# Two transformer layers in float32 on one core: another order of instructions at both ends of the two later attentions

## The chip, the cores and the metric

The kernel runs on one core of a Trainium2 chip. The metric is the device time of one execution in microseconds (us), the median of several runs. The engines are TensorE (PE in the profile, its weight loads apart as PEld), VectorE (DVE), ScalarE (ACT), GpSimd (POOL) and the queue that issues the DMAs (SP). Each runs its own list of instructions in order; semaphores tie the lists together.

## The reference

4096 tokens (2 sequences of 2048) of 256 numbers go through three blocks, all in float32. Block A is attention over a window of 128 with 16 heads and an MLP with GELU, followed by a layer norm of input plus output. Then come two layers B, each an attention with 8 heads of 64 and rotated keys and queries, and a gated MLP:

```python
def _layer(x, wqkv, qs, ksc, wo, lg, lb, w1, b1, w2, b2):
    h = shift_token(x)
    qkv = h @ wqkv
    ...
    q = l2norm(q) * qs
    k = l2norm(k) * ksc
    q, k = rotary_xpos(q, k)
    o = local_attention(q, k, v)
    ...
    x = x + o @ wo
    h = shift_token(x)
    mu = h.mean(-1, keepdims=True)
    var = h.var(-1, keepdims=True)
    h = (h - mu) / jnp.sqrt(var + 1e-05) * lg + lb
    h = h @ w1 + b1
    a, g = jnp.split(h, 2, axis=-1)
    h = a * jax.nn.gelu(g, approximate=False)
    x = x + h @ w2 + b2
    return x
```

After the two layers there is again a layer norm of input plus output.

## The kernel before

A matmul of float32 is made of three products of numbers split into a high and a low part (`product3`, L612 to L614). The tokens of an attention are worked in 32 chunks of 128 (`NCH` = 32), those of an MLP in 8 groups of 512 (`NGRP` = 8).

**The loop of the later attentions.** `pe_attention`, `dve_attention`, `act_attention`, `pool_attention` and `sp_attention` each run over steps s = -3 to 33 (`b_steps`). The order of the work of a step is written out by hand, and it is one order per engine, with exceptions for the first and the last steps. A chunk n goes through: scores (L916), the maxima of the masked scores on DVE in two halves of four heads, `maxima(n, 0)` and `maxima(n, 1)` (L1370), exponentials on ACT (L1876), transposes of the probabilities on PE (`transpose_probs`, L929) and their copies out of PSUM by ACT and DVE (`copy_probs`), the product with the values (L948), a scaling by the inverse row sums (`scale_o`, L1396), the output projection (`out_project`) and the residual (`add_residual`, L1403). Beside that run the projections and rotations of the next chunks: sums of squares (`norms`, L1320), the rotation of the keys on POOL (`rotate_k`) and the inverse norms there (`inverse_norms`, L2103 and L2105), the scaling of the rotated keys and queries on DVE (`scale_rotated`, L1345), their transposes on PE (L890) and the low parts `k_t_low` and `q_t_low` (L1349, L1354). The inverse row sums (`invert_sums`, L1383 and L1387) go through memory: SP stores them (L445) and spreads them (L454).

**Into the MLP.** Step 30 of SP issues, behind `store_inverse(30)` (L445), the load of the first group of the MLP into `g_in0` (L506 to L508), whose memory holds the rotation's tables until then. The beginning of the MLP is woven into steps 31 to 33 as "openings": `norm_stats` (opening 0, L1516 to L1523), `normalize` into `g_z` (opening 1, L1528), eight transposes on PE (L1053), `gain_bias` into `g_h32` (opening 2, L1535), the high part on ACT (`h_high`, L1949), the low parts on POOL (L2148) and DVE, and the first hidden matmuls on PE. One wait matters: `out_project(29)` writes a bank that still holds the scores of chunk 31, so PE waits for both halves of its maxima:

```python
elif n == NCH - 3:
    pe.wait_ge(S["max_ready"], 2 * (g0 + NCH))
```

**Out of block A.** The layer norm behind the last group of block A's MLP (`finish_stats`, L1590 to L1597, and `finish`, L1609) stands in steps -1 and 0 of the attention of layer 0. Layer 1's attention has no such work in it.

## Time and profile before

| | |
|---|---|
| median of 3 runs | 1761.75 us (1761.7 to 1763.97) |
| profiled execution, its own time | 1759.69 us |
| its span | 1757.9 us |
| PE, DVE, ACT, POOL busy | 96%, 82%, 67%, 60% |
| chain that ended last | PE 84%, DVE 9%, ACT 3%, issue 3%, DMA 1% |
| attention of block A, PE busy | 334.32 of 351 us |
| layer 0: start, middle, end of the attention, PE busy | 22.18 of 26, 331.71 of 333, 27.13 of 33 us |
| layer 1: the same | 24.15 of 27, 331.71 of 333, 26.09 of 32 us |

The chain is followed back from the last instruction to what released each one, so its shares say what the end waited for, whereas a busy share says only how much an engine had to do. The stretches of the lower rows were cut by hand at 568, 594, 927 and 960 us, and at 1160, 1187, 1520 and 1552 us.

### The profile page before, as it was taken

What the parts mean: (1) busy time and instruction counts of PE and PEld (TensorE: products, weight loads), DVE (VectorE), ACT (ScalarE), POOL (GpSimd) and SP (SyncE); (2) the same over time, 40 slices, a digit from 0 to 9 for tenths busy, and PEclk for the clock granted to TensorE, in tenths of its full rate; (3) what the DMA queues carried; (4) which work ended last, traced back from release to release, by engine and by line L of the source; (5) the groups of instructions that cost most, each with busy time, mean ns of one, the idle gap of its engine ahead of it and who ended that gap; (6) DMA issues with size and microseconds to landing.
All of it is one profiled execution on the core that took longest, in us unless ns stands there. A gap on an engine that the chain in (4) does not pass through costs nothing.

```text
span 1757.9 us, 43282 instructions
## 1 busy us (share of the span) xinstructions
PE 1695.5 (96%) x15168; PEld 1460.7 (83%) x15168; DVE 1446.6 (82%) x3686; ACT 1170.4 (67%) x3024; POOL 1052.0 (60%) x1052
## 2 busy tenths in 40 slices
PE   6999999989999999999998999999999999999997
PEld 4777777779998788888887888878888888888886
DVE  6888988868887999989997655579999999967776
ACT  6999888855544778878775343367787787743332
POOL 3676566534334687887774444367878777634333
PEclk9999999999999999999999999999999999999999
DMA  3111211022322322222223313122222222131221
GB/s 109 38 38 38 65 38 35 26 103 66 117 72 65 98 81 66 76 76 66 80 67 89 107 54 99 54 92 75 80 63 81 72 70 81 56 111 60 73 84 37
DMA packets 174626, 125.44 MB, mean 71 GB/s; under 512 B 20824, under 2 KB 173664, under 8 KB 173664
## 3 DMA queue, kind: packets, MB, share of 16 engines
q1 hardware_dynamic: 174432, 122.98, 23.0%
q8 instruction: 106, 1.74, 0.4%
q14 instruction: 88, 0.72, 0.1%
HBM read 88.32 MB, written 34.61 MB: 70 GB/s over the span
## 4 chain that ended last, share of the span: by engine, by line
PE 84%; DVE 9%; ACT 3%; issue 3%; DMA 1%; POOL 0%; SPq 0%; POOLq 0%; DVEq 0%; ACTq 0%
PE psum L612 18%; PE psum L614 17%; PE psum L613 17%; PE psum L948 6%; PE psum L916 5%; PE psum L929 5%; PE psum L727 3%; PE psum L709 3%; PE psum L890 3%; ACT a_probs L1757 2%; PE psum L662 1%; DVE a_neg_max L1240 1%; DVE psum L1238 1%; PE psum L699 1%; PE psum L1053 1%
## 5 line engine op out<-in xcount | busy, mean ns | idle before, releaser
L1876 ACT ACTIVATE b_probs<-masked,neg_max 128x256 f32<-128x256 f32 (+1 forms) x512 | 249.8, 489 | 119.4 <-DVE neg_max L1370 119.4
L612 PE MATMUL psum<-wa_hi,b_h_hi 128*128 128x512 f32 (+1 forms) x576 | 234.4, 407 | 6.0 <-DVE wa_lo L1167 3.6
L614 PE MATMUL psum<-wa_hi,b_h_lo 128*128 128x512 f32 (+1 forms) x576 | 214.1, 372 | 0.0
L613 PE MATMUL psum<-wa_lo,b_h_hi 128*128 128x512 f32 (+1 forms) x576 | 214.0, 372 | 0.0
L1370 DVE CUSTOM_DVE_ANT_0 masked<-psum,mask 128x256 f32<-128x256 f32 (+1 forms) x512 | 177.2, 412 | 41.1 <-PE psum L916 40.2
L612 PE MATMUL psum<-g_h_hi,wm_hi 128*128 128x512 f32 (+1 forms) x480 | 190.3, 397 | 3.5 <-POOL g_h_lo L2148 2.4
L2105 POOL TENSOR_TENSOR g_in<-g_in,minus_half 128x16 f32<-128x16 f32 x64 | 187.7, 2933 | 5.3
L614 PE MATMUL psum<-g_h_hi,wm_lo 128*128 128x512 f32 (+1 forms) x480 | 189.2, 394 | 0.0
L613 PE MATMUL psum<-g_h_lo,wm_hi 128*128 128x512 f32 (+1 forms) x480 | 189.2, 394 | 0.0
L1962 ACT ACTIVATE gate<-psum,vec_b 128x512 f32<-128x512 f32 x96 | 66.0, 687 | 153.6 <-PE psum L614 153.5
L612 PE MATMUL psum<-wm_hi,u_hi 128*128 128x256 f32 x576 | 164.5, 286 | 0.1
L614 PE MATMUL psum<-wm_hi,u_lo 128*128 128x256 f32 x576 | 162.9, 283 | 0.0
L613 PE MATMUL psum<-wm_lo,u_hi 128*128 128x256 f32 x576 | 162.6, 282 | 0.0
L1757 ACT ACTIVATE a_probs<-psum,a_neg_max 128x128 f32<-128x128 f32 x512 | 148.1, 392 | 4.6 <-DVE a_neg_max L1240 4.4
L1494 POOL TENSOR_TENSOR g_in<-g_z,g_in 128x512 f32<-128x512 f32 x62 | 80.4, 1297 | 117.6 <-DVE g_in L1320 112.4
L2039 POOL TENSOR_SCALAR_AFFINE_SELECT p_before<-p_now 128x512 f32<-128x512 f32 x120 | 76.3, 636 | 119.2 <-ACT p_now L1767 119.2
L929 PE MATMUL psum<-ident,b_probs 128*128 128x128 f32 x992 | 129.8, 273 | 4.8 <-ACT b_probs L1876 4.6
L612 PEld LDWEIGHTS psum<-wa_hi,b_h_hi 128*128 128x128 f32 x576 | 109.3, 190 | 27.9 <-issue 11.2
L929 PEld LDWEIGHTS psum<-ident,b_probs 128*128 128x128 f32 x992 | 113.4, 140 | 16.1 <-ACT b_probs L1876 8.2
L2144 POOL TENSOR_TENSOR g_rstd<-g_ve,minus_half 128x4 f32<-128x4 f32 x24 | 24.6, 1023 | 170.2 <-DVE g_ve L1523 170.2
L614 PEld LDWEIGHTS psum<-wa_hi,b_h_lo 128*128 128x128 f32 x576 | 109.0, 189 | 20.5
L948 PE MATMUL psum<-b_pt,v_tok 128*64 128x128 f32 x1984 | 122.5, 276 | 0.0
(167 smaller groups left out, 5432.6 us busy)
## 6 DMA issues: line engine op xcount, KB each, us to landing
b_inv_t<-inverse_rows SPq DMA_DIRECT2D x128, 128.0 KB, 3.0
x_mid<-y_out SPq DMA_DIRECT2D x96, 128.0 KB, 2.3
rope_in<-in_rope SPq DMA_DIRECT2D x64, 128.0 KB, 2.4
x_res<-x_state SPq DMA_DIRECT2D x64, 128.0 KB, 2.8
g_in<-x_mid SPq DMA_DIRECT2D x32, 256.0 KB, 3.7
w_raw<-in_w_mlp_b SPq DMA_DIRECT2D x2, 2154.0 KB, 9.1
x_in<-in_x SPq DMA_DIRECT2D x32, 128.0 KB, 2.2
x_res<-in_x SPq DMA_DIRECT2D x32, 128.0 KB, 2.2
```

The lines of the kernel that those rows point to most:

```text
L612: nc.tensor.matmul(out, a_hi, b_hi, start=first, stop=False)
L613: nc.tensor.matmul(out, a_hi, b_lo, start=False, stop=False)
L614: return nc.tensor.matmul(out, a_lo, b_hi, start=False, stop=last)
L916: mm = nc.tensor.matmul(outs[b], q[rows, t, :], k[rows, t, at, :], start=first, stop=last)
L929: mm = nc.tensor.transpose(bank[4 + 2 * r + k // 2][:, at:at + P], b_probs[:, r, k, half, :], ident[:])
L948: mm = nc.tensor.matmul(O[rows, t * P:t * P + P], v_tok[m % U][:, h * 64:h * 64 + 64], b_pt[:, r, 2 * j + b, half, :], start=(m == blocks[ ...
L1370: ins = nc.vector.tensor_tensor_reduce(out[:, at], src[:, at], (mask if now else mask0)[:, at], -1.0, BIG, ALU.add, ALU.min, neg_max[:, r, ...
L1494: engine.tensor_tensor(cos_part[i][:].rearrange("p (h d) -> p h d", d=64), x, table(2 * i, 0, 64), ALU.mult).then_inc(done, 1)
L1757: ins = nc.scalar.activation(a_probs[:, i % 2, k, :], bank[4 + 2 * (i % 2) + b][:, at:at + P], ACT.Exp, bias=a_neg_max[:, n % 2, r, k:k + ...
L1876: ins = nc.scalar.activation(out, src, ACT.Exp, bias=neg_max[:, r, k:k + 1], scale=-1.0, accum_out=row_sum[:, n % 2, 4 * r + k:4 * r + k + 1])
L2039: nc.gpsimd.affine_select(before, now, [[0, 4], [-1, P]], ALU.is_ge, 0.0, base=-1, channel_multiplier=1)
L2105: nc.gpsimd.tensor_tensor(rnorm[:], norm2c[:], minus_half[:], ALU.pow).then_inc(S["rnorm_ready"], 1)
```

## The change

Six things change, none of which alters a result.

In step 30 of both attentions PE runs `out_project(28)` ahead of the first transposes of probabilities, and `transpose_probs(30, 1)` behind the transposes of the rotated keys and queries; DVE and ACT copy `probs(30, 1)` behind the low and high parts, and DVE scales the rotated chunk 31 right behind its rotation. In step 31 DVE runs `norm_stats` of the MLP between the two halves of the maxima. ACT makes the high part of the MLP's first group in two halves, and POOL starts its low part when the first half is there. In step 0 of both attentions DVE runs the two `norms` of chunk 2 behind `q_t_low(1)`. Block A's last layer norm is cut up on DVE: two statistics in step -1, two and the rest in step 0, two scalings at the end of step 1 and two at the end of step 2; its inverse root on POOL moves to step 1, its store on SP to step 3. Two tiles of the attention swap places in memory (`b_inv_t` and an empty space), with the waits that belong to that.

```diff
@@ sp_attention
+                if g0 + n == 0:
+                    sp.wait_ge(MA["f_sum"], NGRP)
+                elif n == 0:
+                    sp.wait_ge(MB["store"], 32 * NGRP + 32)
...
-                if s == 0 and layer == 0:
+                if s == 3 and layer == 0:
                     sp_mlp(sp, MLP_A, MA, None, opening="last")
@@ pe_attention
-                if s == NCH - 1:
+                if s in (NCH - 2, NCH - 1):
                     out_project(s - 2)
...
-                if s == NCH - 2:
-                    out_project(s - 2)
-                if b_chunk(s):
+                if b_chunk(s) and s != NCH - 2:
                     transpose_probs(s, 1)
...
+                if s == NCH - 2:
+                    transpose_probs(s, 1)
@@ dve_attention
                 if b_chunk(s):
                     maxima(s, 0)
+                if s == NCH - 1:
+                    dve_mlp(v, MLP_B, MB, layer, opening=0)
+                if b_chunk(s):
                     maxima(s, 1)
                 if s == NCH - 1:
-                    dve_mlp(v, MLP_B, MB, layer, opening=0)
                     add_residual(s - 2)
                 if b_chunk(s + 1) and s + 1 > 0:
                     rotate_q(s + 1)
+                if s in (0, NCH - 2):
+                    scale_rotated(s + 1)
                 if s == 0:
-                    scale_rotated(s + 1)
                     h_low(s + 3)
-                    if layer == 0:
-                        dve_mlp(v, MLP_A, MA, None, opening="finish")
...
-                if b_chunk(s + 2) and s + 2 > 1:
+                if b_chunk(s + 2) and s + 2 > 2:
                     norms(s + 2, 1)
-                if b_chunk(s):
+                if b_chunk(s) and s != NCH - 2:
                     copy_probs(s, 1)
-                if s == 0:
-                    norms(s + 2, 0)
...
+                if s == NCH - 2:
+                    copy_probs(s, 1)
...
-                if b_chunk(s + 2) and s + 2 > 2:
+                if s == 0:
+                    norms(s + 2, 1)
+                if b_chunk(s + 2) and s + 2 > 1:
                     norms(s + 2, 0)
+                if layer == 0 and s in (-1, 0, 1, 2):
+                    dve_mlp(v, MLP_A, MA, None, opening=("finish", s))
@@ act_mlp
+            def h_high_halves(t):
+                for k, done in ((0, "h_hi_first"), (1, "h_hi")):
+                    a.wait_ge(S["h32_ready"], t * KD + k + 1)
+                    nc.scalar.activation(g_h_hi[:, k, :], g_h32[:, k, :], ACT.Copy).then_inc(S[done], 1)
```

DVE at the last chunk, in both attentions (`ISA` is a maximum of one head and the read of it, `g_stats` and `g_mv` the MLP's statistics, `y_out` the residual of chunk 29). Before, from the last head's maximum:

```order
L1370 ISA masked,neg_max<-psum,mask 128x256
L1370 ISA neg_max 128x1
L1516 BN_STATS g_stats<-g_in 128x6 x4
L1520 BN_AGGR g_mv<-g_stats 128x2 x4
L1523 TENSOR_SCALAR g_ve<-g_mv 128x4
L1403 TENSOR_TENSOR y_out<-psum,x_res 128x256
L1396 TENSOR_TENSOR b_o<-psum,b_inv_t 128x512
L1383 RECIPROCAL b_inv<-row_sum 128x8
L1387 STREAM_TRANSPOSE b_inv_turned<-b_inv 128x32
L1528 TENSOR_SCALAR g_z<-g_in,g_mv,g_rstd 128x256 x4
```

Now, from the fourth head's maximum to the fifth's:

```order
L1375 ISA masked,neg_max<-psum,mask 128x256
L1375 ISA neg_max 128x1
L1524 BN_STATS g_stats<-g_in 128x6 x4
L1528 BN_AGGR g_mv<-g_stats 128x2 x4
L1531 TENSOR_SCALAR g_ve<-g_mv 128x4
L1375 ISA masked,neg_max<-psum,mask 128x256
L1375 ISA neg_max 128x1
```

The statistics moved ahead of four maxima; what follows the maxima (residual, scaled output, inverse sums, `g_z`) has kept its order.

DVE in step 0 of layer 0's attention, from the low part of chunk 3 (`b_h_lo`; `f_` and `g_fin` are block A's last layer norm, the sums over `k_sq` and `q_sq` the norms of chunk 2). Before:

```order
L1312 TENSOR_TENSOR b_h_lo<-psum,b_h_hi 128x256
L1609 TENSOR_SCALAR g_fin<-g_sum,f_mv,f_rstd 128x256 x4
L1485 COPY b_pt<-psum 128x2x128
L1383 RECIPROCAL b_inv<-row_sum 128x8
L1387 STREAM_TRANSPOSE b_inv_turned<-b_inv 128x32
L1320 TENSOR_REDUCE g_in<-k_sq 128x8
L1485 COPY b_pt<-psum 128x2x128
L1320 TENSOR_REDUCE g_in<-q_sq 128x8
L1349 TENSOR_TENSOR k_t_lo<-psum,k_t_hi 128x4x128
L1354 TENSOR_TENSOR q_t_lo<-psum,q_t_hi 128x512
```

Now:

```order
L1317 TENSOR_TENSOR b_h_lo<-psum,b_h_hi 128x256
L1493 COPY b_pt<-psum 128x2x128
L1388 RECIPROCAL b_inv<-row_sum 128x8
L1392 STREAM_TRANSPOSE b_inv_turned<-b_inv 128x32
L1493 COPY b_pt<-psum 128x2x128
L1354 TENSOR_TENSOR k_t_lo<-psum,k_t_hi 128x4x128
L1359 TENSOR_TENSOR q_t_lo<-psum,q_t_hi 128x512
L1325 TENSOR_REDUCE g_in<-k_sq 128x8
L1325 TENSOR_REDUCE g_in<-q_sq 128x8
L1684 BN_STATS f_stats<-g_sum 128x6 x2
L1688 BN_AGGR f_mv<-f_stats 128x2 x4
L1691 TENSOR_SCALAR f_ve<-f_mv 128x4
```

The four scalings left this step, the norms of chunk 2 moved from ahead of the low parts to behind them, and half of the statistics with their aggregation came in at the end. Layer 1 has the same without the `g_fin` and `f_` rows.

## Rows read from the trace of the kernel before

**Rows 1.** Windows: stretch, its length, busy of each engine, granted clock, DMA share, GB/s

```profile
927.00:960.00 33.00, 27.13 (x274) 23.76 (x273) 27.01 (x82) 20.78 (x55) 15.31 (x13) 1.00 0.40 115
...
1520.00:1552.00 32.00, 26.09 (x270) 22.90 (x269) 26.56 (x81) 18.62 (x52) 13.75 (x12) 1.00 0.40 112
573.00:576.00 3.00, 1.46 (x11) 0.90 (x9) 2.83 (x7) 3.00 (x13) 0.18 (x1) 1.00 0.49 179
577.00:579.00 2.00, 2.00 (x7) 1.81 (x8) 1.97 (x8) 1.42 (x4) 0.00 (x0) 0.50 0.00 0
```

**Rows 2.** The chain that ended last, 940 to 960 us: start, length, what

```profile
941.51 0.57 SPq L445
...
943.18 4.71 DMA g_in<-x_mid
...
947.92 1.42 DVE g_stats L1516 x4
...
949.88 0.09 DVE y_out L1403
...
951.20 1.33 DVE g_z L1528 x4
...
953.84 1.54 DVE g_h L1535 x2
...
955.40 1.07 ACT g_h_hi L1949
...
956.54 1.78 POOL g_h_lo L2148
...
958.46 0.47 PE psum L612
```

**Rows 3.** Timeline of DVE: start, length, instruction, in brackets idle before and releaser

```profile
921.62 0.42 DVE L1370 CUSTOM_DVE_ANT_0 masked<-psum,mask 128x256 f32<-128x256 f32 x1 [0.58 <-PE psum L916]
...
939.72 1.29 DVE L1345 TENSOR_TENSOR g_in<-g_in 128x512 f32<-128x512 f32 x2
...
944.80 0.43 DVE L1370 CUSTOM_DVE_ANT_0 masked<-psum,mask 128x256 f32<-128x256 f32 x1 [1.12 <-PE psum L916]
...
947.21 0.42 DVE L1370 CUSTOM_DVE_ANT_0 masked<-psum,mask 128x256 f32<-128x256 f32 x1
```

**Rows 4.** The page's groups: count, busy us, mean ns, idle before

```profile
L1876 ACT ACTIVATE b_probs<-masked,neg_max 128x256 f32<-128x256 f32 (+1 forms) x512 | 249.8, 489 | 119.4 <-DVE neg_max L1370 119.4
```

**Rows 5.** Timeline of PE, the same stretch

```profile
947.69 0.39 PE L612 MATMUL psum<-wa_hi,b_o_hi 128*128 128x256 f32 x1 [0.32 <-DVE neg_max L1370]
...
949.21 1.04 PE L929 MATMUL psum<-ident,b_probs 128*128 128x128 f32 x8
```

**Rows 6.** Timeline of PE, layer 0's attention: first scores of chunks 0 and 2

```profile
568.37 0.33 PE L916 MATMUL psum<-k_t_hi,q_t_hi 64*128 64x128 f32 x2
...
592.90 0.39 PE L916 MATMUL psum<-k_t_hi,q_t_hi 64*128 64x256 f32 x2
```

**Rows 7.** Timeline of PE, layer 1's attention: the same two

```profile
1163.85 0.33 PE L916 MATMUL psum<-k_t_hi,q_t_hi 64*128 64x128 f32 x2
...
1185.65 0.39 PE L916 MATMUL psum<-k_t_hi,q_t_hi 64*128 64x256 f32 x2
```

**Rows 8.** Timeline of DVE, layer 1's chunks 0 and 1

```profile
1171.02 0.65 DVE L1320 TENSOR_REDUCE g_in<-k_sq 128x8 f32<-128x512 f32 x1
...
1180.86 1.28 DVE L1345 TENSOR_TENSOR g_in<-g_in 128x512 f32<-128x512 f32 x2
```

**Rows 9.** Timeline of POOL, the same stretch

```profile
1171.83 1.29 POOL L1494 TENSOR_TENSOR g_in<-g_z,g_in 128x512 f32<-128x512 f32 x1 [0.86 <-DVE g_in L1320]
...
1176.16 2.93 POOL L2105 TENSOR_TENSOR g_in<-g_in,minus_half 128x16 f32<-128x16 f32 x1
```

**Rows 10.** Timeline of DVE, layer 0's chunk 0

```profile
568.47 1.40 DVE L1590 BATCH_NORM_STATS2 f_stats<-g_sum 128x6 f32<-128x256 f32 x4
...
575.90 1.76 DVE L1609 TENSOR_SCALAR g_fin<-g_sum,f_mv,f_rstd 128x256 f32<-128x256 f32 x4
```

More of the change, by code:

```diff
@@ L1448, in dve_attention @@
                     copy_probs(s, 0)
-                if b_chunk(s + 1) and s + 1 > 1:
+                if b_chunk(s + 1) and s + 1 > 1 and s != NCH - 2:
                     scale_rotated(s + 1)
@@ L1668, in dve_mlp @@
                 h_low(base)
-            if opening == "finish_stats":
-                finish_stats(base + NGRP - 1, 1)
-            if opening == "finish":
-                finish(base + NGRP - 1, 1)
+            last, z = NGRP - 1, g_sum[1]
+            if opening == ("finish", -1):
+                v.wait_ge(S["f_sum"], NGRP)
+                for i in range(2):
+                    nc.vector.bn_stats(f_stats[:, i, :], z[:, i, :])
+            if opening == ("finish", 0):
+                for i in range(2, 4):
+                    ins = nc.vector.bn_stats(f_stats[:, i, :], z[:, i, :])
+                ins.then_inc(S["f_stats"], 1)
+                v.wait_ge(S["f_stats"], 2 * last + 1)
+                for i in range(4):
+                    ins = nc.vector.bn_aggr(f_mv[:, i, :], f_stats[:, i, :])
+                ins.then_inc(S["f_stats"], 1)
+                v.wait_ge(S["f_stats"], 2 * last + 2)
+                nc.vector.tensor_scalar_add(f_ve[:], f_mv[:, :, 1], EPS).then_inc(S["f_var"], 1)
+            if opening == ("finish", 1):
+                v.wait_ge(S["store"], last * 32 + 32)
+                v.wait_ge(S["f_rstd"], NGRP)
+            if opening in (("finish", 1), ("finish", 2)):
+                half = opening[1] - 1
+                for i in range(2 * half, 2 * half + 2):
+                    ins = nc.vector.tensor_scalar(g_fin[:, i, :], z[:, i, :], f_mv[:, i, 0:1], f_rstd[:, i:i + 1],
+                                                  ALU.subtract, ALU.mult)
+                ins.then_inc(S[("f_stats", "fin_ready")[half]], 1)
             if opening is not None:
@@ L1924, in act_attention @@
                     h_high(s + 3)
-                if b_chunk(s):
+                if b_chunk(s) and s != NCH - 2:
                     copy_probs(s, 1)
@@ L1994, in act_mlp @@
                 high(base, 0)
+            elif opening and c is MLP_B:
+                h_high_halves(base)
             elif opening:
@@ L2121, in pool_attention @@
             for s in b_steps():
-                if s == 0 and layer == 0:
-                    pool_mlp(pool, MLP_A, MA, None, opening="finish")
                 if b_chunk(s - 2):
@@ L2136, in pool_attention @@
                     split_low(pool, nc.gpsimd, w_raw, wm_lo, wm_hi, wm_hi_done, wm_split, MLP_B.WCOLS, (s - 5) // 2, layer + 1)
+                if s == 1 and layer == 0:
+                    pool_mlp(pool, MLP_A, MA, None, opening="finish")
                 if b_chunk(s + 2) and s + 2 > 1:
@@ L2146, in h_low @@
             def h_low(t):
-                pool.wait_ge(S["h_hi"], t + 1)
+                if c is MLP_B and t % NGRP == 0:
+                    pool.wait_ge(S["h_hi_first"], layer + 1)
+                else:
+                    pool.wait_ge(S["h_hi"], t + 1)
                 nc.gpsimd.tensor_tensor(g_h_lo[:, 0, :], g_h32[:, 0, :], g_h_hi[:, 0, :].bitcast(F32),
```

19 lines of the change are left out of this document (10 added, 9 removed).

## The prediction

> **What bounds the kernel now.** I read the windows first. In the middle of both later attentions PE is busy all the time, so a change at their ends can only win or lose what PE sits idle there: 5.9 us in the window around the end of layer 0's attention and 5.9 us at layer 1's [rows 1]. Then I read the chain through that end. It leaves PE at SP's store of the inverse sums (941.51), goes over the three loads of `g_in` behind it, waits for their landing (the last issue is at 943.18, the landing 4.71 us later, at 947.89), and runs on through the MLP's statistics at 947.92, `g_z`, `g_h32`, its high part, its low part, and the first hidden matmul at 958.46 [rows 2]. The reader is to see that the statistics already start the moment that their data land. The timeline of DVE says the rest: its last maximum starts at 947.21 and lasts 0.42, so the eight maxima of chunk 31, which began at 944.80, fill the wait for the load almost to the end [rows 3]. Last come the starts. From the first score of chunk 0 to that of chunk 2 layer 0 takes 592.90 - 568.37 = 24.5 us [rows 6] and layer 1, which has no layer norm to finish, 1185.65 - 1163.85 = 21.8 us [rows 7].
>
> **The statistics between the halves of the maxima.** This is the term that decides. The load stands on SP behind `store_inverse(30)`, which waits for `invert_sums(30)` on DVE. In the new order the same pieces stand ahead of `invert_sums(30)` as before (two maxima halves, `rotate_q`, `scale_rotated`, `scale_o`, a copy), in another order, and nothing on SP moved at that step. So the data still land at about 947.9. Before, the four maxima of a half took (947.21 - 944.80) / 7 x 4 = 1.38 us [rows 3], so the first half was over at 946.2, and the low parts of chunk 31, which now no longer stand behind a copy of 0.6, let it be over some 0.7 us earlier. That gain is void: DVE then sits with the statistics at the head of its queue until 947.9, 2.4 us. The statistics take from 947.92 to 949.88 [rows 2], and only then comes the second half of the maxima, whose last one now ends at 949.88 + 1.38 + 0.1 = 951.4 where it ended at 947.6.
>
> Queued behind that are four exponentials on ACT, 4 x 489 ns = 2.0 us [rows 4], hence over at 953.4, and `out_project(29)` on PE, whose first matmul started at 947.69, released by the last maximum [rows 5]. PE's list is in order, so it stands idle from the end of the value product at 947.69 - 0.32 - 0.7 = 946.7 to 951.4, 4.7 us in one piece. `out_project(29)` takes 949.21 - 947.69 = 1.5 us [rows 5], so it ends at 952.9, and the residual on DVE can start at 953.1. From that residual to `g_z` it was 951.20 - 949.88 = 1.3 us [rows 2]; `g_z` is now at 954.4, 3.2 us later than before. The exponentials are not the bound there: the inverse sums come up at 954.0. From `g_z` to `g_h32` it stays 953.84 - 951.20 = 2.6 us [rows 2].
>
> **The high part in halves.** From `g_h32` to the hidden matmul it was 958.46 - 953.84 = 4.6 us. Now POOL starts after half of `g_h32` (0.8 of 1.54) and half of the high part (0.6 of 1.07), and its 1.78 and three hand-overs of 0.25 together stay [rows 2]: 3.4 us, a gain of 1.2. Sum for one end: 3.2 - 1.2 = 2.0 us late. PE alone comes to the same: behind the transposes of `g_z` it has `values(31)` and `out_project(30)`, so it could not start the hidden matmul sooner. I take **+2.1 us at each end, +4.2** for both; the second end is built alike, with the same waits [rows 1]. Bounds: if PE's own work is what counts, 2.0; if the exponentials push the inverse sums, 2.6.
>
> **The clock of PE.** In the trace of before the granted clock falls once inside the kernel's middle: at the start of layer 0's attention PE was busy less than half of 573 to 576, and from 577 to 579 the clock was 0.50, that is 1.2 instead of 2.4 GHz [rows 1]. At the ends of the attentions PE waits in pieces of 1 to 2 us, and the clock stayed at 1.00 [rows 1]. An idle piece of 4.7 us is longer than what preceded that fall, so I expect it there, at both ends. What is slow then is `out_project(29)`, on which the residual waits: 1.5 us of matmuls become at most 3.0. The bounds are 0 (no fall) and 1.5 plus 1.1 for the eight transposes of `g_z` if they are caught too; I take 1.2, since the slow spell may begin before the work and end within it. **+2.4** for both. The Trainium skill (TensorE: Matmul & The Clock Gate, "The HAM clock gate (the "warmup" mystery)") says that the cold spell is a matter of time and not of a number of matmuls; by that rule a spell that begins in the idle piece is partly spent before any matmul runs, and the two together could cost as little as 1 us. The trace cannot tell which, as its one spell caught running matmuls.
>
> **Step 30.** `out_project(28)` fills a wait of PE for exponentials, and the low parts come 0.7 us earlier. As said, the landing swallows it: 0. The new order has `scale_rotated(31)` reach its inverse norms just as POOL has them; a stall there of 0.1 would move the load by as much.
>
> **The start of layer 1's attention.** The norms of chunk 2 started at 1171.02 [rows 8]; behind a copy and the low parts they start at about 1173.5. POOL waits for them: from its first instruction of `rotate_k(2)` at 1171.83 to the end of the power at 1176.16 + 2.93 it takes 7.3 us [rows 9], so the inverse norms come at about 1181.6. `scale_rotated(2)` on DVE, at 1180.86 before [rows 8], would come up at 1180.6 and waits 1 us. Its transposes, the low part behind it and `project_v(3)` on PE, each a hair behind DVE already, are late by that. Less the 0.2 that the scores of chunk 1 gain: **+0.8 us**. Bounds 0 (if hidden behind PE) and 1.1.
>
> **The start of layer 0's attention.** It loses what it had over layer 1, 24.5 - 21.8 = 2.7 us, since the maxima of chunk 0 no longer wait behind four statistics (1.40), and the copies behind four scalings (1.76) [rows 10]. It gets the same +0.8. Two statistics and the aggregation, some 1.3 us, now delay the maxima of chunk 1, but the wait for the inverse norms swallows all but 0.2. The scalings, 0.9 us at the ends of steps 1 and 2, fall into DVE's idle piece of 0.58 per step [rows 3]; what is over, 0.3 to 0.4, PE loses. Sum: -2.7 + 0.8 + 0.2 + 0.3 = **-1.4 us**. Bounds -2.7 and 0. The store moved to step 3 of SP is two issues in a step that has time, and no load waits for it before step 6.
>
> **Sum.** +4.2 + 2.4 + 0.8 - 1.4 = +6.0 us. Made against the profiled execution of 1759.69 us it gives 1765.7; that execution was 2.1 us under the median of 1761.75, so against the median it is **1767.8 us**, 0.34% slower. No change of this kernel under 0.2%, 3.5 us, can be told from none.
>
> **Rivals.**
> (1) All as said, but the clock holds, or falls at one end only: 1765.4 to 1766.6. For it: the clock held through the waits at both ends before. Against: none was nearly so long.
> (2) The load is there in time, and the change is not slower. This is one mechanism with one place: if `g_in` landed by 945.5, DVE would not stop, the second maxima would be over at 948.9, `g_z` at about 952.0, and the hidden matmul, with the halves' 1.2 us, at 958.1 instead of 958.46. With the starts: -0.7 + 0.8 - 1.4 = -1.3 us, 1760.5. Each end breaks even at a landing of 945.8, the whole at 946.1. Against it stands 947.89 and an issue that nothing moved.
> (3) The norms of chunk 2 cost nothing and the clock holds, so that only the stall remains: 0 for layer 1 and -2.2 for layer 0, so 1761.75 + 4.2 - 2.2 = 1763.8, no measurable change.
> (4) The start of layer 0 gains nothing, because the finishing work in steps 0 to 2 delays DVE there as much as it did, or the clock falls there still: 1769 to 1770.5.
>
> **How the numbers follow.** The forecast 0.60, with its own range 1766.6 to 1769.2; (1) 0.15; (2) 0.07; (3) 0.08; (4) 0.10. The bounds of the two starts and of the clock widen the range to both sides: 1763.3 to 1769.8, which leaves out (2), what of (3) lies lower, and the top of (4). Slower by over 0.2% means above 1765.3: forecast, (4) and most of (1), 0.83. Within: the rest of (1), (3) and part of (2), 0.13. Faster, below 1758.2, needs (2) with both starts at their best bound: 0.04.
>
> **What the changed profile would show.** Right: `g_stats` on DVE with some 2.4 us idle ahead of it, released by the load; four maxima behind it; `out_project(29)` on PE with 4.7 us idle ahead of it, released by DVE; a window behind it with the clock near 0.5; POOL's `g_h_lo` starting before the high part is complete; `scale_rotated(2)` idle ahead of POOL's power; 22.5 to 23.5 us between the scores of chunk 0 and 2 in layer 0. Wrong: a landing of `g_in` well before 946 (then rival 2), or a hidden matmul less than 1 us late at each end.

## The result, and the profile after

The changed kernel takes 1773.84 us (median of 6 runs, 1771.12 to 1774.63), the kernel before 1762.08 us beside it: the ratio is 1.0065, 95% interval [1.0054, 1.0076]. The profiled execution took 1772.48 us, its span is 1770.6 us, 12.7 more than before. The forecast of 1767.8 had the sign and the main mechanism right; the loss is twice as large.

The page's groups that answer to those of before: the exponentials last as long each as they did [rows 4], but ACT waits 10 us more for maxima in front of them.

```profile
L1904 ACT ACTIVATE b_probs<-masked,neg_max 128x256 f32<-128x256 f32 (+1 forms) x512 | 249.8, 489 | 129.2 <-DVE neg_max L1375 129.2
```

So the exponentials did not grow; the wait ahead of them did. By the same page DVE is busy for 1451.7 us (1446.6 before) and PE for 1699.9 (1695.5), so single instructions of theirs took longer too; which, the rows below show. The windows of the ends of both attentions, and three inside layer 0's end:

```profile
928.00:961.00 33.00, 24.98 (x233) 22.65 (x234) 24.48 (x78) 18.05 (x52) 11.20 (x11) 0.90 0.31 91
1528.00:1561.00 33.00, 25.11 (x246) 22.54 (x246) 25.53 (x80) 18.74 (x54) 12.82 (x12) 0.95 0.33 90
```

```profile
949.00:953.40 4.40, 0.00 (x0) 0.00 (x0) 3.33 (x17) 0.00 (x0) 1.01 (x1) 0.90 0.79 233
953.40:959.70 6.30, 6.20 (x30) 6.20 (x31) 3.25 (x12) 2.68 (x10) 0.00 (x0) 0.53 0.14 43
952.50:959.34 6.84, 5.84 (x27) 5.84 (x28) 3.79 (x15) 2.67 (x9) 0.61 (x1) 0.50 0.24 74
```

PE does nothing for the whole of the first of these, and in the 6.3 us behind it its granted clock is 0.53, the lower level (1.2 GHz) for nearly all of it. The last of the three windows holds the whole slow stretch: it runs from about 952.5, 1 us ahead of the first matmul, to about 959.3. Before, the clock was 1.00 over the whole end [rows 1]. The chain that ended last, through the same end:

```profile
942.83 0.57 SPq L446
...
944.51 5.47 DMA g_in<-x_mid
950.00 1.42 DVE g_stats L1524 x4
...
951.98 0.42 DVE masked L1375
...
953.50 0.58 PE psum L617
...
956.43 3.23 PE psum L934 x16
959.66 0.89 PE psum L1058 x8
...
960.64 1.54 DVE g_h L1543 x2
...
964.30 0.47 PE psum L617
```

Set beside [rows 2]: between the statistics and `g_z` there stood a piece of 0.09 of the residual; now PE stands in the chain with `out_project(29)` and 16 transposes of probabilities at half clock. The timeline of DVE there:

```profile
946.37 0.42 DVE L1375 CUSTOM_DVE_ANT_0 masked<-psum,mask 128x256 f32<-128x256 f32 x1
950.00 1.41 DVE L1524 BATCH_NORM_STATS2 g_stats<-g_in 128x6 f32<-128x256 f32 x4 [3.21 <-DMA g_in<-x_mid]
...
956.47 0.42 DVE L1408 TENSOR_TENSOR y_out<-psum,x_res 128x256 f32<-128x256 f32 x1 [3.02 <-PE psum L619]
...
957.76 1.34 DVE L1536 TENSOR_SCALAR g_z<-g_in,g_mv,g_rstd 128x256 f32<-128x256 f32 x4
```

and of PE at both ends:

```profile
953.50 0.58 PE L617 MATMUL psum<-wa_hi,b_o_hi 128*128 128x256 f32 x1 [5.59 <-DVE neg_max L1375]
...
1553.27 0.58 PE L617 MATMUL psum<-wa_hi,b_o_hi 128*128 128x256 f32 x1 [4.68 <-DVE neg_max L1375]
```

Now the starts. Layer 1's took 21.80 us from the scores of chunk 0 to those of chunk 2 [rows 7] and takes 1194.52 - 1169.71 = 24.81. The timelines of DVE, of POOL and of PE, layer 1's chunk 2:

```profile
1183.31 1.48 DVE L1502 TENSOR_TENSOR g_in<-g_h,g_in 128x512 f32<-128x512 f32 x1
...
1187.94 1.81 DVE L1350 TENSOR_TENSOR g_in<-g_in 128x512 f32<-128x512 f32 x2 [0.54 <-POOL g_in L2142]
```

```profile
1182.94 1.29 POOL L2134 TENSOR_TENSOR g_in<-g_in,k_sq 128x512 f32<-128x512 f32 x1
1184.19 0.70 POOL L2140 TENSOR_SCALAR g_in<-g_in 128x16 f32<-128x16 f32 x1
1184.98 2.93 POOL L2142 TENSOR_TENSOR g_in<-g_in,minus_half 128x16 f32<-128x16 f32 x1
```

```profile
1189.81 1.09 PE L895 MATMUL psum<-ident,g_in 128*128 128x128 f32 x8 [2.05 <-DVE g_in L1350]
```

The reader is to see three things: the forecast wait for POOL's power (0.54), two instructions of DVE that are longer than they were (1.81 where it was 1.28 [rows 8], and 1.48 where the same instruction takes 0.69 in a kernel below), and a wait of PE of 2.05 that comes of all of it. In layer 0 the four scalings of block A's layer norm, 1.76 us together before [rows 10], have become two pairs of 1.84 and 2.50 us. Timeline of DVE, then of POOL beside it:

```profile
591.60 1.84 DVE L1698 TENSOR_SCALAR g_fin<-g_sum,f_mv,f_rstd 128x256 f32<-128x256 f32 x2
...
604.70 2.50 DVE L1698 TENSOR_SCALAR g_fin<-g_sum,f_mv,f_rstd 128x256 f32<-128x256 f32 x2
```

```profile
604.47 1.30 POOL L2134 TENSOR_TENSOR g_in<-g_in,k_sq 128x512 f32<-128x512 f32 x1
605.72 1.34 POOL L2148 TENSOR_TENSOR b_o_lo<-b_o,b_o_hi 128x512 fp32r<-128x512 f32 x1
```

In layer 0 the scores of chunks 0, 2 and 4 on PE stand at:

```profile
568.17 0.33 PE L921 MATMUL psum<-k_t_hi,q_t_hi 64*128 64x128 f32 x2
...
591.33 0.39 PE L921 MATMUL psum<-k_t_hi,q_t_hi 64*128 64x256 f32 x2
...
618.24 0.39 PE L921 MATMUL psum<-k_t_hi,q_t_hi 64*128 64x256 f32 x2
```

From chunk 0 to chunk 2 that is 23.16 us, 1.37 less than before [rows 6] and inside the 22.5 to 23.5 that were forecast; from chunk 2 to chunk 4 it is 26.91, where the kernel before has 24.27 (its scores of chunk 4 follow here). So the start wins at first, and loses more than that in the two steps where the scalings now stand.

To find the loss in each kernel I measure four stretches on PE: layer 0's start (scores of chunk 0 to those of chunk 4), each end (scores of chunk 30 to the first hidden matmul), and layer 1's start (scores of chunk 0 to chunk 2). The rows of before that they need beyond those shown, timeline of PE:

```profile
617.17 0.39 PE L916 MATMUL psum<-k_t_hi,q_t_hi 64*128 64x256 f32 x2
...
932.75 0.39 PE L916 MATMUL psum<-k_t_hi,q_t_hi 64*128 64x256 f32 x2
...
1525.47 0.39 PE L916 MATMUL psum<-k_t_hi,q_t_hi 64*128 64x256 f32 x2
...
1551.22 0.47 PE L612 MATMUL psum<-g_h_hi,wm_hi 128*128 128x512 f32 x1 [1.22 <-POOL g_h_lo L2148]
```

| kernel | median, us | layer 0 start | layer 0 end | layer 1 start | layer 1 end |
|---|---|---|---|---|---|
| before | 1762.1 to 1762.7 | 48.80 | 25.71 | 21.80 | 25.75 |
| changed | 1773.84 | 50.07 | 30.46 | 24.81 | 29.32 |
| changed, statistics back | 1764.64 | 50.03 | 26.32 | 24.51 | 24.83 |
| changed, norms back | 1769.58 | 49.61 | 29.80 | 21.79 | 29.02 |
| changed, layer norm back | 1774.10 | 49.56 | 30.48 | 24.80 | 29.19 |
| changed, statistics and norms back | 1761.73 | 49.64 | 24.94 | 21.80 | 25.41 |
| changed, load first | 1766.84 | 50.09 | 26.60 | 24.34 | 26.08 |
| changed, norms back, load first | 1762.95 | 49.62 | 25.69 | 21.81 | 26.71 |
| changed, second scalings later | 1773.06 | 49.08 | 30.44 | 24.80 | 29.42 |
| before, statistics alone | 1771.81 | 49.47 | 30.77 | 21.81 | 28.74 |
| before, norms alone | 1764.93 | 49.59 | 26.33 | 24.65 | 25.49 |
| before, halves alone | 1760.81 | 49.43 | 24.79 | 21.80 | 24.99 |
| before, step 30 alone | 1762.18 | 48.81 | 26.54 | 21.80 | 26.63 |
| before, halves, step 30, load first | 1757.25 | 49.43 | 24.03 | 21.81 | 23.81 |

The changed kernel against before: 1.27 + 4.75 + 3.01 + 3.57 = 12.6 us, the whole of the 12.7 by which the spans differ; between the stretches nothing is lost. One caution: a stretch can differ between traces in which nothing of it was changed. Layer 0's start takes 48.8 in two such traces and 49.4 to 49.5 in three, with the slow stretch of the clock at 576 to 582 in the first and at 583 to 588 in the others, so of its 1.27 us only 0.6 to 1.3 are the change's. Layer 0's end takes 26.33 instead of 25.71 with the norms alone, which do not touch it: the granted clock was 0.50 there from 945.3 to 948.6. And the trace of before is of an execution 2 to 3 us under the medians beside the other kernels, so losses come out larger by the stretches than by the medians, and gains smaller.

### The profile page after: what moved, and what is told of

Read it like the earlier page. It is cut to its first block, busy times and chain, and to the rows that moved or that the text cites. A ratio compares the mean times of both kernels' runs of the same rounds, so it can differ in the third digit from the quotient of the medians.

```text
span 1770.6 us, 43285 instructions
## 1 busy us (share of the span) xinstructions
PE 1699.9 (96%) x15168; PEld 1464.4 (83%) x15168; DVE 1451.7 (82%) x3686; ACT 1170.9 (66%) x3026; POOL 1052.6 (59%) x1052
## 4 chain that ended last, share of the span: by engine, by line
PE 83%; DVE 9%; ACT 4%; issue 3%; DMA 1%; POOL 0%; SPq 0%; POOLq 0%; DVEq 0%; ACTq 0%
PE psum L617 18%; PE psum L619 17%; PE psum L618 17%; PE psum L953 5%; PE psum L934 5%; PE psum L921 5%; PE psum L732 3%; PE psum L714 3%; PE psum L895 3%; ACT a_probs L1785 2%; PE psum L667 1%; DVE a_neg_max L1245 1%; DVE psum L1243 1%; PE psum L704 1%; DVE masked L1375 1%
```

## The experiments

The verdicts are ratios to the kernel before, timed beside them, with 95% intervals.

**Where the loss sits.** The statistics back behind both halves of the maxima, in the changed kernel:

```diff
                 if b_chunk(s):
                     maxima(s, 0)
+                    maxima(s, 1)
                 if s == NCH - 1:
                     dve_mlp(v, MLP_B, MB, layer, opening=0)
-                if b_chunk(s):
-                    maxima(s, 1)
```

> The changed kernel with norm_stats put back behind both halves of the maxima of chunk 31; all else as changed. Theory (the statistics stand at the head of DVE's queue until the load lands, and out_project(29) and the exponentials queue behind them): the ends, 4.75 and some 3.8 us late in the changed kernel, lose all of that and keep the 1.2 us of the halves each, so about 11 us come back: 1763 us, and out_project(29) has no idle piece of 5 us ahead of it; the granted clock stays at 1.00 there. Rival (the ends are late because of the new order of step 30 or a longer load): less than 3 us come back, 1771 or more.

Measured 1764.64 us, ratio 1.0011 [1.0002, 1.0020]: 9.2 us come back. The ends fall from 30.46 to 26.32 and from 29.32 to 24.83. The expected clock of 1.00 did not hold at layer 0's end: it fell there for some 3 us (0.57 and 0.58 in two windows of 2 us) although no wait of 5 us was left, and that end came back less; how much of that is the clock's was not measured apart. The theory stands: most of the loss is this one move. Beside it ran the same move alone on the kernel before:

> The kernel before with one part of the change alone: norm_stats of the MLP between the two halves of the maxima of chunk 31. Blind forecast's own term: 3.2 us an end, and 1.2 more for the clock, 8.8 us in sum: 1770.8 us. Theory from the changed trace (the halves' 1.2 us taken off 4.75 and 3.8): 5 to 6 us an end, 1772 to 1774 us, so that this part alone is as slow as the whole change. Rival (the ends' loss needs the new order of step 30 with it): under 1766 us.

Measured 1771.81 us, 1.0051 [1.0038, 1.0065], 9.0 us slower with an interval of 6.7 to 11.5. So this move makes most of the slowdown alone, and needs no other part of the change; the third answer is out. The forecast's 8.8 and the lower part of the other's 10 to 12 lie inside the interval, and the two ends, 5.06 and 2.99 us longer, make 8.05, nearer to the forecast. The second end is of use for more: PE idles in one piece there too, but its clock did not fall. PE and a window in this kernel:

```profile
1552.57 0.38 PE L612 MATMUL psum<-wa_hi,b_o_hi 128*128 128x256 f32 x1 [3.86 <-DVE neg_max L1370]
```

```profile
1546.00:1564.00 18.00, 11.83 (x131) 10.56 (x129) 11.79 (x40) 8.72 (x22) 5.21 (x5) 1.00 0.54 155
```

So the stall by itself costs 3.0 us an end, where 3.2 was forecast. At layer 0's end of the same kernel the idle piece is 4.61 and the clock was at 0.50 from 953.4 to 960.2.

**The norms.** Put back in the changed kernel:

```diff
@@ dve_attention
-                if b_chunk(s + 2) and s + 2 > 2:
+                if b_chunk(s + 2) and s + 2 > 1:
                     norms(s + 2, 1)
                 if b_chunk(s) and s != NCH - 2:
                     copy_probs(s, 1)
+                if s == 0:
+                    norms(s + 2, 0)
```

> The changed kernel with the norms of chunk 2 put back in their old places of step 0 (norms(2, 1) ahead of the second copy, norms(2, 0) behind it); all else as changed. Theory (the late norms hold back POOL's power and shift POOL's work beside DVE's, which slows both): layer 1's start gives back its 3.0 us, layer 0's another 1 to 3, so 1767.8 to 1769.8 us, with 22 us from the scores of chunk 0 to those of chunk 2 in layer 1. Rival (the blind price of 0.8 us for each start was right and the rest of layer 1's 3.0 us comes from the clock): 1772 to 1773 us and layer 1's stretch above 24 us.

Measured 1769.58 us, 1.0045 [1.0032, 1.0059]: 4.3 us come back, and layer 1's start is 21.79 us, what it was before to the hundredth. The timeline of DVE in this kernel, the same two instructions as above:

```profile
1183.22 0.69 DVE L1502 TENSOR_TENSOR g_in<-g_h,g_in 128x512 f32<-128x512 f32 x1
...
1186.42 1.28 DVE L1350 TENSOR_TENSOR g_in<-g_in 128x512 f32<-128x512 f32 x2
```

and of POOL beside them:

```profile
1181.42 0.24 POOL L2140 TENSOR_SCALAR g_in<-g_in 128x16 f32<-128x16 f32 x1
1181.74 2.93 POOL L2142 TENSOR_TENSOR g_in<-g_in,minus_half 128x16 f32<-128x16 f32 x1
```

`rotate_q(2)` starts at nearly the same place in both kernels, 13.8 us behind the scores of chunk 0 with the norms back and 13.6 with them late. With the norms in time POOL is by then in its power of 16 numbers a partition, and DVE needs 0.69; with the norms late POOL is in an addition of 512 numbers, and DVE needs 1.48. What follows `scale_rotated(2)` starts 1189.67 - 1169.71 = 19.96 us behind those scores instead of 18.20, 1.8 later: 0.8 of rotation, 0.54 of wait and 0.53 of the scaling itself, less 0.1 of everything before. The other 1.2 us of the 3.0 I put down to PE's clock, which no run here separates from the wait: it was at 0.74 from 1190 to 1193 behind the wait of 2.05, and at 1.00 over the whole stretch with the norms back. The norms late alone, on the kernel before:

> The kernel before with one part alone: the two norms of chunk 2 behind q_t_low(1) in step 0 of both attentions. Blind forecast's term: 0.8 us a start: 1764.3 us. Theory from the changed trace (3.0 us at layer 1: 0.8 in rotate_q and 0.5 in scale_rotated, both slowed beside POOL's wide instructions, a wait of 0.5 for the power, and PE's slow clock behind a wait of 2.05): layer 1's start takes 24.8 us, layer 0's grows by 0.5 to 1.5: 1766 to 1767.5 us.

Measured 1764.93 us, 1.0015 [1.0006, 1.0024]: 2.6 us slower, interval 1.1 to 4.2. By the time this cannot be told from the forecast's 1.6, and it lies under what I expected from the trace. Stretch by stretch the trace has it: layer 1's start 24.65, 2.85 longer and far from 0.8, with PE waiting the same 2.05 us; layer 0's start 49.59, 0.8 longer than before, of which an unchanged start can show up to 0.7. In the changed kernel the norms cost layer 0's start 50.07 - 49.61 = 0.5. So layer 0 pays the forecast 0.8 or less, and the price above the forecast is paid in layer 1.

**The layer norm of block A.** Put back whole in the changed kernel (POOL's inverse root and SP's store, not shown, go back to step 0 with it):

```diff
@@ dve_attention
                 if s == 0:
                     h_low(s + 3)
+                    if layer == 0:
+                        dve_mlp(v, MLP_A, MA, None, opening="scalings")
...
-                if layer == 0 and s in (-1, 0, 1, 2):
-                    dve_mlp(v, MLP_A, MA, None, opening=("finish", s))
+                if layer == 0 and s == -1:
+                    dve_mlp(v, MLP_A, MA, None, opening=("finish", -1))
+                    dve_mlp(v, MLP_A, MA, None, opening=("finish", 0))
```

> The changed kernel with block A's last layer norm put back whole: four statistics and the aggregation in step -1, four scalings in step 0, the power on POOL in step 0, the store on SP in step 0; all else as changed. Blind forecast: cutting it up was worth 2.2 us, so 1776 us. Theory from the trace (the cut-up scalings take 1.84 and 2.50 us a pair beside POOL's work where they took 0.84 before, so that cutting up won little): 1773 to 1774.5 us, within 1 us of the changed kernel. The four scalings then take about 0.42 us each.

Measured 1774.10 us, 1.0069 [1.0056, 1.0083], 0.3 us above the changed kernel: cutting it up is worth nothing that can be told, where I had forecast 2.2. That nothing is a gain and a loss: with the layer norm whole the scores of chunk 2 follow those of chunk 0 after 25.30 us instead of 23.16, and those of chunk 4 follow chunk 2 after 24.26 instead of 26.91. Cutting it up wins 2.1 us in the first two steps and loses 2.65 in the next two. The timeline of DVE:

```profile
576.36 1.77 DVE L1709 TENSOR_SCALAR g_fin<-g_sum,f_mv,f_rstd 128x256 f32<-128x256 f32 x4
```

Four scalings in 1.77 us at their old place, against 4.34 in the new ones. Whether it is POOL's neighbourhood that slows them there, the next kernel asks:

```diff
@@ dve_attention
                 if b_chunk(s):
                     maxima(s, 1)
+                if s == 3 and layer == 0:
+                    dve_mlp(v, MLP_A, MA, None, opening=("finish", 2))
...
-                if layer == 0 and s in (-1, 0, 1, 2):
+                if layer == 0 and s in (-1, 0, 1):
```

> The changed kernel with the last two scalings of block A's layer norm moved on DVE from the end of step 2, beside POOL's product with the tables, to behind the maxima of chunk 3, beside POOL's power; the first two stay. Theory (DVE's scalings, memory to memory, are slowed by POOL's wide instructions on the same memory and not by its power of 16 numbers): this pair takes 0.8 to 0.9 us instead of 2.50, PE's wait of 1.09 for the exponentials of chunk 3 goes, 1 us comes back: 1772.8 us. Rival (the scalings are slow wherever they stand there, for example because they are the first to read that memory, or POOL slows them in its power too): the pair takes 1.8 us or more, no gain.

The timeline of DVE, then of POOL:

```profile
610.99 0.74 DVE L1700 TENSOR_SCALAR g_fin<-g_sum,f_mv,f_rstd 128x256 f32<-128x256 f32 x2
```

```profile
609.71 0.25 POOL L2142 TENSOR_SCALAR g_in<-g_in 128x16 f32<-128x16 f32 x1
610.04 2.93 POOL L2144 TENSOR_TENSOR g_in<-g_in,minus_half 128x16 f32<-128x16 f32 x1
```

The pair takes 0.74 instead of 2.50 us. Layer 0's start falls from 50.07 to 49.08 us, the microsecond that was expected, and the wait of 1.09 ahead of the transposes of chunk 3 is gone. The time, 1773.06 us, 1.0056 [1.0044, 1.0069], is 0.8 lower, which by itself says nothing; the trace decides, and it decides for contention with POOL's wide instructions. The trace of before, where nothing was moved, bears it out. It has 64 such scalings, 0.41 us each in the median, and the ones that meet a wide instruction of POOL take up to 1.39; four of block A, and POOL beside them:

```profile
412.91 3.25 DVE L1609 TENSOR_SCALAR g_fin<-g_sum,f_mv,f_rstd 128x256 f32<-128x256 f32 x4 [0.98 <-POOL f_rstd L2175]
```

```profile
412.78 2.58 POOL L1167 TENSOR_TENSOR wa_lo<-w_raw,wa_hi 128x512 fp32r<-128x512 f32 x2
```

In every such meeting of four traces (before, changed, layer norm back, second scalings later) the scaling ends 0.15 to 0.16 us behind POOL's instruction: the one at 591.60 in the changed kernel takes 1.52 us with POOL's ending at 592.97, the one at 595.17 in the last kernel 0.69 with POOL's ending at 595.71, and each is followed by one of 0.40 that met none. It is held until POOL is done, not slowed in proportion. (That first pair is shorter in the last kernel than in the changed one, 1.01 against 1.84, though nothing of it was moved. The kernels with the statistics back and with the load first have it at 1.01 to 1.04 too, and their start at 50.03 and 50.09, so the microsecond is the second pair's.)

The Trainium skill (SBUF — State Buffer, "Who interferes with whom") says that DVE and GpSimd share one pair of ports, that a DVE instruction with two inputs in SBUF contends with a GpSimd instruction that reads SBUF, that `tensor_scalar` can run in a mode that takes the pair too, and that DVE instructions with at most one SBUF input outside these modes do not. The traces agree in kind: 1.48 against 0.69 for a product of two tiles in SBUF, 2.50 against 0.74 for two scalings, and no maximum of the attention, whose other operand is in PSUM, over 0.43 in 512, whatever POOL did. They do not agree for POOL's power: it reads SBUF as well, and the product and the scalings beside it ran at full speed; there the measurement decides.

**The small parts alone.** The high part in halves, on the kernel before:

```diff
@@ act_mlp
+            elif opening and c is MLP_B:
+                h_high_halves(base)
@@ pool_mlp, h_low
+                if c is MLP_B and t % NGRP == 0:
+                    pool.wait_ge(S["h_hi_first"], layer + 1)
```

> The kernel before with one part alone: the high part of the MLP's first group in two halves, POOL starting after the first. Blind forecast's term: 1.2 us an end, 2.4 in sum: 1760.0 us beside 1762.4 for the kernel before. Rival (PE is not free for the hidden matmul, values(31) and out_project(30) stand before it, or DVE's and POOL's low parts, now side by side, slow each other and eat the gain): 1761.5 to 1762.4, no change.

Measured 1760.81 us, 0.9990 [0.9981, 0.9999]. The ends are 0.92 and 0.76 us shorter, not 1.2. DVE's low part is longer than it was; DVE, then POOL beside it:

```profile
959.23 1.15 DVE L1541 TENSOR_TENSOR g_h_lo<-g_h,g_h_hi 128x512 fp32r<-128x512 f32 x1 [0.70 <-ACT g_h_hi L1954]
```

```profile
958.55 1.28 POOL L2158 TENSOR_TENSOR g_h_lo<-g_h,g_h_hi 128x512 fp32r<-128x512 f32 x1 [1.38 <-ACT g_h_hi L1954]
```

It now starts 0.7 behind POOL's and runs beside it, and takes 1.15 where it took 0.69 in the trace of before; the rival's second half was right, for a third of the gain. Step 30 alone (in part; the copies of `probs(30, 1)` on DVE and ACT move with it):

```diff
@@ pe_attention
-                if s == NCH - 1:
+                if s in (NCH - 2, NCH - 1):
                     out_project(s - 2)
@@ dve_attention
-                if s == 0:
+                if s in (0, NCH - 2):
                     scale_rotated(s + 1)
```

> The kernel before with one part alone: the new order of step 30 on PE, DVE and ACT. Blind forecast's term: 0, since the load's landing decides the end: 1762.4 us within 1 us. Rival (the order makes the inverse sums, and with them SP's store and the load behind it, later, so that part of the end's loss is step 30's): 1764 to 1766.

Measured 1762.18 us, 0.9998 [0.9989, 1.0007]: no change that can be told, as forecast. The trace leans the other way by 0.83 and 0.88 us at the ends, 1.7 in sum. At layer 0's end the last issue of the load stands 10.66 us behind the scores of chunk 30 (10.43 before) and the statistics start 15.99 behind them (15.17 before). At layer 1's end the statistics start where they did, and the granted clock was 0.50 from 1548.0 to 1551.3. By the interval a loss of up to 1.2 us is possible; more is not settled.

**Do they add?** Statistics and norms both back in the changed kernel:

> The changed kernel with both the statistics and the norms of chunk 2 in their old places; the halves, step 30 and the cut-up layer norm stay as changed. Theory (the two losses are separate and add: 9.2 us and 4.3 us as measured one by one): 1773.8 - 13.5 = 1760.3 us, 0.1% under the kernel before, which cannot be told from it. Rival (they share a cause, such as the clock falling once whatever stands there, so that undoing one has given back part of the other): 1762 to 1764 us.

Measured 1761.73 us, 0.9998 [0.9989, 1.0007]. The interval is 1760.8 to 1763.9 us, so the plain sum, 1760.3, lies just outside it: undoing both gives back 12.1 us and not 13.5. By the stretches it is 12.9 against 9.0 and 4.4 one by one, 0.5 us less than the sum. The two losses are separate for nine tenths. For the rest there is a plain candidate: of the 4.4, 0.96 are at the two ends, which the norms do not touch. In the kernels with the new step 30 and the load behind the store, the statistics can start between 15.4 and 16.4 us behind the scores of chunk 30 at layer 0's end, and between 15.0 and 15.8 at layer 1's, without any change there. With both undone no difference to the kernel before is left.

**The load itself.** Nothing above shows directly that the landing sets the end. So the order on SP, in the changed kernel:

```diff
@@ sp_attention
-                if b_chunk(s):
-                    store_inverse(s)
                 if s == NCH - 2:
                     sp_mlp(sp, MLP_B, MB, layer, opening="first")
+                if b_chunk(s):
+                    store_inverse(s)
```

> The changed kernel with one move on SP: in step 30 the three loads of the MLP's first group stand ahead of the store of the inverse sums of chunk 30 instead of behind it. They then wait for the rotation of chunk 31, over at about 941.2, and not for the inverse sums (SP's store at 942.83). Theory (the landing of the load sets the end, microsecond for microsecond): the landing comes 1.5 us earlier and the changed kernel gains that at each end, 3 us in sum: 1770.8 us. Rival (the end is set by PE's own work and the slow clock, not by the landing): 1773 to 1774.

Measured 1766.84 us, 1.0020 [1.0011, 1.0030]: 7.0 us gained, more than twice what I expected, so the rival is out and my size too. The timeline of SP:

```profile
944.24 0.37 SPq L511 DMA_DIRECT2D g_in<-x_mid  x1
...
945.20 0.51 SPq L513 DMA_DIRECT2D g_in<-x_mid  x1
945.81 0.57 SPq L446 DMA_DIRECT2D inverse_rows<-b_inv_turned  x1
```

and of DVE and PE in this kernel:

```profile
949.72 1.40 DVE L1524 BATCH_NORM_STATS2 g_stats<-g_in 128x6 f32<-128x256 f32 x4
```

```profile
953.21 0.39 PE L617 MATMUL psum<-wa_hi,b_o_hi 128*128 128x256 f32 x1 [2.30 <-DVE neg_max L1375]
```

The last issue is 945.20 - 936.86 = 8.34 us behind the scores of chunk 30, which was 944.51 - 933.84 = 10.67. I had counted the wait for the inverse sums, 1.5, and forgotten the store's own issue of 0.68 that stood ahead of the loads. The transfer is shorter as well, 3.79 us from the last issue where it was 5.47, and why is not shown. So the data land 12.1 us behind the scores of chunk 30, 4.0 earlier, and no longer end any wait of DVE: the statistics start 12.86 instead of 16.16 us behind those scores, 3.3 earlier, and the ends shrink by 3.86 and 3.24. PE still waits 2.30, now only for the 2 us of statistics between the maxima, and the clock still fell behind it (0.50 from 953.7 to 957.0). With the norms back as well:

> The changed kernel with the norms of chunk 2 in their old places and the MLP's first load ahead of the store of the inverse sums; the statistics stay between the halves of the maxima. Theory (the two losses are separate and add: 4.3 and 7.0 us as measured one by one): 1773.8 - 11.3 = 1762.5 us. Rival (the clock, which falls behind the wait in one way or another, keeps part of it): 1764 to 1766.

Measured 1762.95 us, 1.0002 [0.9994, 1.0011], as the sum said. With the load in time the ends stand where they did before the change at layer 0 (25.69 against 25.71) and 0.96 us later at layer 1, where PE's clock fell behind the same wait of 2.30. That does not make the new place of the statistics free: these ends also have the halves and the new step 30, and the next kernel shows what they are worth without the statistics between the maxima.

**A better kernel.** From the kernel before, what paid or was free: the halves, step 30, and the load ahead of the store; the statistics stay behind the maxima.

> The kernel before with three parts: the high part in halves, the new order of step 30, and the MLP's first load on SP ahead of the store of the inverse sums of chunk 30; the statistics, the norms and block A's layer norm stay as before. Theory (the landing of the load is what the ends hang on, and step 30 pays only with the load out of the way): no wait for the load at g_stats; each end 0.85 us shorter by the halves and 0.6 to 0.85 by the earlier scores of chunk 31, so 3 to 3.4 us in sum: 1759.0 to 1759.7 us, 0.2% faster than before. Rival (the load first delays the inverse sums, and the end hangs on these instead): 1761 to 1763.

Measured 1757.25 us, 0.9969 [0.9958, 0.9980]: 0.3% faster than before and 16.6 us faster than the changed kernel. That is 5.1 us, interval 3.5 to 7.4, more than the 3 to 3.4 expected; by the stretches it is 3.0, each end 1.7 to 1.9 us shorter and layer 0's start, unchanged, 0.6 longer in this trace. The timeline of DVE:

```profile
948.12 0.42 DVE L1370 CUSTOM_DVE_ANT_0 masked<-psum,mask 128x256 f32<-128x256 f32 x1
948.47 1.41 DVE L1519 BATCH_NORM_STATS2 g_stats<-g_in 128x6 f32<-128x256 f32 x4
```

Statistics follow the last maximum with no idle time, and the granted clock is 1.00 from 940 to 966. Set beside the kernel with the norms back and the load first, in which the order at the ends differs in nothing but the place of the statistics (25.69 and 26.71 against 24.03 and 23.81), it says what that place costs when the load is in time: 1.7 us at layer 0's end, and 2.9 at layer 1's, with the slow clock.

## Why the prediction was right or wrong

**The statistics between the halves: right in mechanism and place.** The wait for the load at the head of DVE's queue, the four maxima and `out_project(29)` behind it, PE's idle piece of 5 us and the slow clock all came as written. The two ends had been put at 3.3 us each with the clock; they measured 4.75 and 3.57. At layer 1's end the pieces fit as well: DVE waits 2.30 (2.4 forecast), PE 4.68 (4.7), and the data land where they did. The end of layer 1 in the statistics-alone kernel shows the stall without a slow clock at 2.99, against 3.2. At layer 0's end two things were mis-sized. The landing, taken as fixed, came 1 us later against the scores of chunk 30 (16.16 against 15.17 us), most of it in the transfer, 5.47 us where it had been 4.71 [rows 2], and 0.23 in the issue, so DVE's wait was 3.21 and PE's 5.59. And the clock's term, 1.2, was too low there.

**The clock.** I had put only `out_project(29)` into the slow spell, since a part of the spell was to be spent idle. At layer 0's end that is half right. The clock fell 1 us before the first matmul, and `out_project(29)` took 956.23 - 953.50 = 2.73 us where it took 1.5, the 1.2 of the forecast. But the spell went on to 959.3 and held 5.8 us of work, so that the 16 transposes of probabilities took 3.23 as well. At layer 1's end it began with the first matmul and ended 3.4 us later. With 2.99 for the stall, 1.0 for the later landing and the halves taken off (0.92 and 0.76), the clock comes to about 1.7 us at layer 0's end and 1.3 at layer 1's; that is an estimate from the stretches. By the Trainium skill (TensorE: Matmul & The Clock Gate, "The HAM clock gate (the "warmup" mystery)") a spell is a matter of time; the traces do not contradict that, and at layer 0's end a part of the spell was spent idle, but the cheap case that I had worked out beside it did not come. That the length of the idle piece decides, as I argued, does not hold: behind two close waits of 1.29 and 1.15, behind one of 2.05 and one of 2.30 the clock fell too, behind one of 3.86 it did not, and behind 2.30 once it fell and once it did not. What exactly draws the line stays open.

**The high part in halves: right, mis-sized.** 1.2 forecast, 0.84 measured, the difference lost where the low parts of DVE and POOL collide.

**Step 30: as forecast**, within 0.2%. The reason given was that the landing swallows its gain; in the last kernel, where the load is out of the way, step 30 and the load together make the ends 0.76 and 1.18 us shorter than the halves alone did.

**The start of layer 1: the step that failed by 2.2 us.** The forecast had the norms late, the wait for POOL's power (1 us forecast) and bounds of 0 and 1.1. The power did come late and there was a wait, 0.54. But I moved POOL's work in time without asking what DVE would run beside it: `rotate_q(2)` and `scale_rotated(2)` lost 0.8 and 0.53 us to POOL's wide instructions, and PE's wait of 2.05 had the slow clock behind it, which the forecast had at nothing here. The upper bound of 1.1 held only as long as durations stayed the same.

**The start of layer 0: the step that failed by 2.7 us.** Forecast -1.4, measured +1.27, of which 0.6 to 1.3 are real. The gain came: 23.16 us from the scores of chunk 0 to those of chunk 2, as forecast (the clock, which fell there before, did not fall in this trace and has a part in it). What failed is the term for the scalings at the ends of steps 1 and 2, put at 0.3 since they would sink into DVE's idle piece of 0.58 a step. From chunk 2 to chunk 4 the start is 2.64 us longer, and with the layer norm back whole that is gone (24.26 against 24.27 before), so it is all theirs. They fell beside POOL's rotation and low part and took 4.34 instead of 1.76 us, DVE had no idle piece left, and PE waited for the exponentials of chunks 2 and 3. This was close to rival (4) (0.10), whose mechanism, finishing work that delays DVE as much as it did, was the true one in its sum, though its price was too low.

**The rivals.** The condition of (2) was made true in the runs with the load first: data at 12.1 us behind the scores of chunk 30, where (2) asked for 945.5 - 932.75 = 12.75. DVE then does not stop, and the ends come to -0.02 and +0.96 against its -0.36 each. That is near it where the clock holds, but it is the halves and step 30 that pay for it; the place of the statistics still costs 1.7 to 2.9 us an end. (1) and (3), in which the clock holds at one end at least, are out: in the changed kernel and in the three others with the same order at the ends it fell at both. In the statistics-alone kernel it held at one.

**The sum.** 12.6 measured by stretches against 6.0 forecast: 2.7 from layer 0's start, 2.2 from layer 1's, 1.45 and 0.27 from the ends. The range ended at 1769.8, 2 us above the forecast, though the upper bounds that the prediction itself gives its terms add up to 5.2 + 5.2 + 1.1 + 0 = 11.5 us, which is 1773.2. So it was too narrow by its own working as well, and the two bounds of the starts were too low besides, since they were worked out with every instruction at its old duration.

## What to carry to other kernels

Before an instruction is put ahead of others in an in-order queue, look at what releases it, and at when that lands; here, in the changed kernel, moving the load paid 7 us, and moving the work that needs it cost 9. When the order changes what runs beside what, a duration from the old trace is no constant: for each moved instruction of DVE that reads two tiles in SBUF, or scales from SBUF to SBUF, ask what POOL does at that time, and put it beside POOL's small instructions. A fresh wait of PE should be priced with the work behind it at half clock as its upper bound.

## What the runs showed of the hardware that was not expected

- Scalings of 128x256 from SBUF to SBUF: 0.74 us for two beside POOL's power of 16 numbers, 2.50 us for the same two beside POOL's addition and subtraction of 512. Products of two SBUF tiles of 128x512: 0.69 against 1.48 us. POOL's wide instructions kept their 1.27 to 1.34 us in these cases, its small one (128x16) went from 0.24 to 0.70. A scaling that met a wide one ended 0.15 to 0.16 us behind it.
- The granted clock of PE stayed at 0.50 for 5.8 us of continuous work behind an idle piece of 5.59 us, having fallen 1 us before that piece ended. It fell behind pieces of 2.05 and 2.30 us as well, and held behind one of 3.86.
- The same three loads of 256 KB took 4.71, 5.47 and 4.57 us from the last issue to landing at places of the same program order (layer 0 before, layer 0 and layer 1 after), and 3.7 to 3.9 at all six ends of the kernels that issue them ahead of the store.
